# Two tiles instead of one fetched row by row by SyncE in every 24 groups of layer 1 (two-layer graph network, one core)

## The chip, the core and the metric

The kernel runs on one core of a Trainium2 chip. The metric is the device time of one execution in microseconds (us), the median of several runs. Five engines work side by side, each on its own list of instructions: TensorE (PE, with its weight loads PEld), VectorE (DVE), ScalarE (ACT), GpSimd (POOL) and SyncE (SP). They meet at semaphores. DMA transfers are issued by POOL and SP here and carried by 16 shared DMA engines.

## The reference

Two message passing layers over a graph of 6250 nodes with 128 features and 206250 edges, sorted by destination. Layer 0 is attention with 8 heads, layer 1 is attention by cosine. Cut to layer 1, which is the layer that changes:

```python
x = x + L0_gnn(edge_index, relu(layernorm(x)), Wq, Wk, Wv, gamma, beta, 8)
h = relu(layernorm(x))
norm  = ||h||                                   # per node
alpha = sum(h[row] * h[col]) / (norm[row] * norm[col]) * beta
alpha = exp(alpha - segment_max(alpha, row)[row])
alpha = alpha / segment_sum(alpha, row)[row]
x = x + segment_sum(alpha[:, None] * h[col], row)
```

For every edge the row `h[col]` has to be fetched from a table in memory by an index.

## The kernel before, in words

The sorted edges are cut into tiles of 128 edges, four tiles (GT = 4) to a group, 417 groups (GROUPS), 1668 tiles. Layer 0 (`layer0_edges`) and layer 1 (`layer1_edges`) both walk over the groups, one step for each group, and every engine walks by itself. In layer 1 the step of group i is:

- POOL (`gather_groups`, L918) fetches the 128 rows of each of its four tiles with one indirect DMA each into `h_rows` (the name `G` in the code), a ring of RING1 = 12 groups. It waits until ACT has copied the indices (`s_idx`) and until PE has used the group that lay in that place of the ring (`s_sum`).
- SP (`step`, L1462 to L1470) fetches at every fourth step the one-hot rows of four groups (`own`, L1467). Before it issues that DMA at step i it waits (L1466) until ACT has widened group i - 9 (`s_hotT`), which ACT does four steps ahead of its own step; so SP can be up to some 12 steps ahead of ACT, and no further. Then come the rows by hand (below), in the same step and on the same queue.
- ACT makes the logits from the cosines (L1507), copies the indices (L1483), scales the one-hot matrices (L1499) and widens `own` (L1494).
- PE multiplies: the queries (L1559), the transposed logits (L1568), the sums (L1578), the maxima (L1586).
- DVE makes the cosines (L1625), the running maxima (L1646, L1662), the differences, the one-hots (L1676) and adds the sums of group i - 9 (L1620).

One tile of every 24 groups (HAND1 = 24) is not gathered by POOL: tile 3 of the group with u = 23, u being the group's number modulo 24. Its 128 rows are fetched one at a time by SP (`hand_rows`, L1459: one DMA of 130 floats for each row) into the buffer `hand`, six rows (BYHAND1) in each of 22 steps, from the step with u = 10 to the step with u = 7 of the next 24. The numbers of the rows are loaded from `hand_ids` into registers, twelve at a time (L1455, 11 loads for a tile). Before the first of the 128 rows SP waits until ACT has emptied the buffer (`s_copied`). ACT copies `hand` into the ring (L1514) at its step u = 21, after waiting for all 128 rows, and DVE waits for that copy before the cosines of the group u = 23. Sixteen tiles (HANDS1 = 16) are fetched so. The first 24 groups have none, and the last tile is in group 407 (16 x 24 + 23).

The row numbers come from a small table in memory, `tile_names`, which SP writes at the start of layer 0 in four DMAs (L1021), before it loads the first rows of layer 0 (L1026). DVE's work in layer 0 starts once they have landed.

DVE, ACT, SP and POOL run their steps in loops whose bodies hold 24 groups in layer 1, PE's holds 12. The first 48 groups (24 or 12 on some engines) and the last are written out.

Of the kernel before, what the change touches and what calls it, by code (L numbers as in the profile page):

```python
# [15 lines left out]
P = 128  # L16
# [31 lines left out]
GT = 4  # L48
# [17 lines left out]
RING1 = 12  # L66
NEAR = 4
SLABS = -(-NT // P)
WHOLE = NT // P
# [6 lines left out]
FOUR = 4  # L76
QUADS = -(-GROUPS // FOUR)
HAND1 = 2 * RING1
HAND1_AT, BYHAND1 = 10, 6
BATCHES1 = -(-P // BYHAND1)  # L80
COPY1_AT = 21
HANDS1 = (GROUPS - HAND1) // HAND1
HAND_EVEN1 = sum(min(BYHAND1, P - BYHAND1 * b) for b in range(0, BATCHES1, 2))
PART = 7
# [4 lines left out]
TW = D + 2  # L89
# [4 lines left out]
i32 = mybir.dt.int32  # L94
# [757 lines left out]
def inside(g):  # L852

    return not isinstance(g, int) or 0 <= g < GROUPS
# [36 lines left out]

def by_hand(u, t, period):

    return period is not None and u == period - 1 and not (isinstance(t, int) and t == 0)


def gathers_of(t, u, ring, period):

    if period is None:
        return GT * (t + 1)  # L900
    each, now = GT * (period // ring), GT * (u // ring + 1)
    if u % ring < ring - 1 or isinstance(t, int) and t == 0:
        return each * t + now
    return (each - 1) * t + now + (u < period - 1)


def gather_groups(pool, ring, table, G, idx, s_idx, s_read, s_gat, s_go, period=None):
# [25 lines left out]
    nc.tensor.matmul(out, pick_row[:, g_u % FOUR, :], rows[:, h, :], start=True, stop=True).then_inc(s_spread, 1)  # L933


def hand_names(dram):

    per, step = P // GT, HAND1 * GT // (P // 4)
    rows = dram["names"].rearrange("k a c -> (k a) c")
    return rows[2 * step - 1:step * (HANDS1 + 1):step, :].rearrange("(o n) c -> o n c", o=1)  # L940


def layer0_edges(nc, mem, dram):

    with ExitStack() as ctx:
# [11 lines left out]
        G = sb("kv_rows", [P, RING0, GT, 2 * D])  # L957
# [4 lines left out]
        rows = sb("rows0", [FOUR, RING0 // FOUR, GE], bf16)  # L962
# [14 lines left out]
        s_ids = sem("s_ids0")  # L977
# [23 lines left out]
        s_sum = sem("s_sum0")  # L1001
# [4 lines left out]
        names = words.bitcast(i32)[:, 0:WHOLE, :]  # L1006
        loc_tiles = dram["loc_rows"].rearrange("g (j e) -> (g j) e", e=P)

        @block.sync
        def _(sp):  # L1010
            for n, (a, b) in enumerate(LOADS):
                sp.dma_start(words[:, a:min(b, WHOLE), :], words_in(dram, a, min(b, WHOLE))).then_inc(s_words[n], 16)
            sp.dma_start(words[0:REST, WHOLE, :], last_words(dram)).then_inc(s_words[n], 16)
            sp.wait_ge(s_bytile, 1)
            sp.dma_start(loc_tiles[0:whole * P, :].rearrange("(k t) e -> t k e", t=P), by_tile[:, 0:whole, :]).then_inc(s_stored, 16)
            sp.wait_ge(s_bytile, 2)
            sp.dma_start(loc_tiles[whole * P:NT, :], by_tile[0:rest, whole, :]).then_inc(s_stored, 16)
            sp.wait_ge(s_decoded, len(LOADS) + 1)
            for a in range(4):
                q = P // 4 * (a + 1) - 1  # L1020
                sp.dma_start(dram["names"][:, a, :].rearrange("(o k) c -> o k c", o=1), names[q:q + 1, :, :]).then_inc(s_ids, 16)  # L1021
            sp.wait_ge(s_ids, 16 * 4)
            sp.wait_ge(s_stored, 32)

            def load_rows(first, h, n):
                sp.dma_start(rows[0:n, h, :], dram["loc_rows"][ds(first, n), :]).then_inc(s_row[h], 16)  # L1026

            def step(i, u, t):
                last = isinstance(i, int) and i == GROUPS - 1
                if inside(i) and (u % FOUR == FOUR - 1 or last):  # L1030
                    q, h, n = RING0 // FOUR * t + u // FOUR, u // FOUR, u % FOUR + 1
                    sp.wait_ge(s_own, i + 1)
                    sp.sem_inc(s_go, 1)
                    sp.dma_start(own_quad(dram, q, n),
                                 own[:, FOUR * h:FOUR * h + n, :].rearrange("p g e -> p (g e)")).then_inc(s_kept[h], 16)
# [97 lines left out]
        def _(dve):  # L1133
# [3 lines left out]
            for n, (a, b) in enumerate(LOADS):  # L1137
                a, b = a * P, min(b * P, NT)
# [5 lines left out]
                                        ALU.add).then_inc(s_local, 1)  # L1144
            nc.vector.tensor_scalar(names, names, KEY, KEYS, ALU.logical_shift_right, ALU.bitwise_and).then_inc(s_decoded, 1)
            dve.wait_ge(s_part, 1)
            dve.wait_ge(s_ids, 16 * 4)

            block_4_back = BlockNumbers(nc, dve, blkid, RING0, IDS0, -4)

# [214 lines left out]
def layer1_edges(nc, mem, dram):  # L1365
# [3 lines left out]
    with ExitStack() as ctx:  # L1369
        def sb(name, shape, dt=f32):  # L1370
            return ctx.enter_context(nc.sbuf_tensor(name, shape, dt))

        def sem(name):
            return ctx.enter_context(nc.semaphore(name))
# [5 lines left out]
        PS = mem["psum"]  # L1380
        G = sb("h_rows", [P, RING1, GT, TW])
        own = sb("own1", [P, RING1, GE], u8)
        hand = sb("hand1", [P, TW])
        ids = sb("hand_ids1", [1, HANDS1 * P], i32)
        idx = sb("idx_ring1", [P, RING1, GT], i32)
        loc_b = sb("loc_b", [P, NT], bf16)
        iota_j = sb("iota_j", [P, P, GT], bf16)
# [24 lines left out]

        s_idx = sem("s_idx1")
        s_ids = sem("s_ids1")
        s_hand = [sem(f"s_hand1_{k}") for k in range(2)]
        s_copied = sem("s_copied1")
        s_gat = [sem(f"s_gat1_{k}") for k in range(RING1)]
        s_own = [sem(f"s_own_{k}") for k in range(RING1 // FOUR)]
# [24 lines left out]
        @block.sync  # L1443
        def _(sp):
            named = {}

            def hand_rows(u, t):
                n, b = (t, u - HAND1_AT) if u >= HAND1_AT else (t - 1, u + HAND1 - HAND1_AT)
                if b >= BATCHES1 or isinstance(n, int) and not 1 <= n <= HANDS1:
                    return  # L1450
                if b == 0:
                    need(sp, s_copied, n - 1)
                a = BYHAND1 * b
                if b % 2 == 0:
                    _, named[0] = nc.values_load_multi_w_load_instructions(  # L1455
                        ids[0:1, ds(P * n - P + a, min(2 * BYHAND1, P - a))], engines=[sp.engine], min_val=0,
                        max_val=NPAD - 1, skip_runtime_bounds_check_because="the numbers that the gathers use")
                for p in range(a, min(a + BYHAND1, P)):
                    sp.dma_start(hand[p:p + 1, :], dram["h1"][ds(named[0][p - a + BYHAND1 * (b % 2)], 1), :]  # L1459
                                 ).then_inc(s_hand[b % 2], 16)  # L1460

            def step(i, u, t):  # L1462
                if u % FOUR == 0 and inside(i):
                    n, k = min(FOUR, GROUPS - i) if isinstance(i, int) else FOUR, u % RING1
                    need(sp, s_hotT, i + n - RING1)
                    sp.sem_inc(s_go, 1)  # L1466
                    sp.dma_start(own[:, k:k + n, :].rearrange("p g e -> p (g e)"),  # L1467
                                 own_quad(dram, HAND1 // FOUR * t + u // FOUR, n)).then_inc(s_own[k // FOUR], 16)
                if inside(i):
                    hand_rows(u, t)  # L1470
            sp.dma_start(ids.rearrange("o (n c) -> o n c", c=P), hand_names(dram)).then_inc(s_ids, 16)
            sp.wait_ge(s_ids, 16)
            walk(sp, step, HAND1, first=0, drain=0, peel=2)

        @block.gpsimd
# [4 lines left out]
        def _(act):  # L1480
# [22 lines left out]
            def step(i, u, t):  # L1503
                if inside(i):
# [2 lines left out]
                    nc.scalar.activation(logit[:, u % RING1, :], cosb[:, u % SOON, :], ACT.Identity,  # L1507
                                         bias=cb[:, 1:2]).then_inc(s_logit, 1)
                    indices(i + RING1, u % RING1)
                if u == COPY1_AT and by_hand(HAND1 - 1, t, HAND1) and inside(i):  # L1510
                    act.wait_ge(s_hand[0], 16 * HAND_EVEN1 * t)
                    act.wait_ge(s_hand[1], 16 * (P - HAND_EVEN1) * t)
                    act.wait_ge(s_sum, HAND1 * t + HAND1 - RING1)
                    nc.scalar.copy(G[:, RING1 - 1, GT - 1, :], hand[:, :]).then_inc(s_copied, 1)  # L1514
                if inside(i - 7):
                    k = (u - 7) % SOON
                    act.wait_ge(s_below, i - 6)
# [74 lines left out]
        def _(dve):  # L1592
# [38 lines left out]
            def step(i, u, t):  # L1631
# [16 lines left out]
                if inside(i):  # L1648
                    dve.wait_ge(s_gat[u % RING1], 16 * gathers_of(t, u, RING1, HAND1))
                    if by_hand(u, t, HAND1):  # L1650
                        dve.wait_ge(s_copied, t)
                    dve.wait_ge(s_q, i + 1)
                    need(dve, s_logit, i + 1 - SOON)
                    need(dve, s_prod, i)
                    cosines(u, 0, GT // 2)
# [59 lines left out]
def program(nc, x, src, dst, wq, wk, wv, gamma, beta, cos_beta, out):  # L1715
# [2 lines left out]
        "offs": nc.dram_tensor("column_offsets", (2, NCHUNK, NBUK * STEP), bf16).ap(),  # L1718
        "loc_rows": nc.dram_tensor("loc_rows", (GROUPS, GE), bf16).ap(),
        "own": nc.dram_tensor("own_rows", (QUADS, P, FOUR * GE), u8).ap(),  # L1720
        "names": nc.dram_tensor("tile_names", (WHOLE, 4, P), i32).ap(),
# [48 lines left out]
```

## Time and profile before

| | |
|---|---|
| median of 3 runs | 4963.15 us (4962.42 to 4964.2) |
| the profiled execution | 4970.87 us |
| its span, first to last instruction | 4969.1 us |
| mean granted TensorE clock | 0.811 of full speed |
| layer 0's gathers | 592.1 to 2697.8 us |
| layer 1's gathers | from 2830.3 us, last one starts at 4905.0 us |
| busy in the span | PE 73%, PEld 60%, DVE 81%, ACT 47%, POOL 71% |

An engine's busy time leaves out its register, branch, semaphore and DMA-issuing instructions; the whole of SP is of that kind, so it has no busy share, and its load has to be read from the times between its DMAs. A figure such as "L1459 ... x2048" in a row counts instructions of one line of the kernel. "Idle before" names what an engine's next instruction came after.

### The profile page before, as it was taken

How to read it: one execution, taken by the hardware profiler on the slowest of the kernel's cores; microseconds unless marked ns; L12 is line 12 of the kernel's file. 1: busy time of each engine (PE TensorE's matmuls, PEld its weight loads, DVE VectorE, ACT ScalarE, POOL GpSimd, SP SyncE). 2: the span in 40 equal slices, each digit the busy share in tenths (PEclk: the TensorE clock that was granted, in tenths of full speed). 3: DMA queues.
4: the chain of work that ended last, by engine and by line, in shares of the span. 5: the costliest groups of instructions: out<-in, count | busy, mean ns of one | idle time of the engine just before them, and what ended most of it. 6: DMA issues, size and time to landing. Idle time of an engine off the chain costs nothing. (4 is left out here: it accounts for less than half of the span.)

```text
span 4969.1 us, 105610 instructions
## 1 busy us (share of the span) xinstructions
PE 3613.5 (73%) x21325; PEld 2995.8 (60%) x21326; DVE 4026.9 (81%) x12159; ACT 2349.1 (47%) x8244; POOL 3505.2 (71%) x3613
## 2 busy tenths in 40 slices
PE   5777577877777777777775177777778777777776
PEld 1444455655555655555664077777777777667775
DVE  7999688888888888888888677777777777777776
ACT  3999511111111111111111676776766777777774
POOL 1667677777777777777775177777777777777773
PEclk7999687677777777777776588998988999999887
DMA  1000134334333333333332222222222222222222
GB/s 50 21 29 28 43 114 119 117 116 117 117 117 119 117 117 117 117 117 119 117 117 86 46 69 68 68 68 68 69 67 68 68 69 68 67 68 70 68 68 54
DMA packets 206558, 412.52 MB, mean 83 GB/s; under 512 B 66973, under 2 KB 97984, under 8 KB 206206
## 3 DMA queue, kind: packets, MB, share of 16 engines
q0 software_dynamic: 136384, 329.69, 24.5%
q1 hardware_dynamic: 67986, 75.70, 4.8%
q10 hardware_dynamic: 1836, 4.03, 0.3%
q14 instruction: 326, 2.67, 0.2%
q8 instruction: 26, 0.43, 0.0%
HBM read 363.48 MB, written 42.44 MB: 82 GB/s over the span
## 5 line engine op out<-in xcount | busy, mean ns | idle before, releaser
L918 POOL DMA_INDIRECT h_rows<-h_table,idx_ring x1652 | 1572.1, 952 | 635.2 <-issue 487.8
L918 POOL DMA_INDIRECT kv_rows<-kv_table,idx_ring x1668 | 1598.5, 958 | 513.8 <-issue 506.3
L1127 PE MATMUL psum<-vx,hot 128*128 128x136 f32 x3336 | 820.9, 387 | 413.3 <-DVE acc L1158 400.2
L1127 PEld LDWEIGHTS psum<-vx,hot 128*128 128x128 f32 x3336 | 628.7, 260 | 584.2 <-DVE acc L1158 555.7
L1080 ACT ACTIVATE vx<-clip 128x32 f32<-128x32 f32 x417 | 95.8, 230 | 1741.5 <-DVE clip L1200 1741.5
L1620 DVE SCALAR_TENSOR_TENSOR h_sb<-h_sb,corr,psum 128x129 f32 x1668 | 582.3, 349 | 391.0 <-PE psum L1578 145.6
L1116 PE MATMUL psum<-q_sb,hotT 128*128 x3336 | 679.7, 367 | 75.6 <-DVE prod L1173 65.3
L1116 PEld LDWEIGHTS psum<-q_sb,hotT 128*128 128x128 f32 x3336 | 578.1, 261 | 210.8 <-issue 210.8
L1568 PE MATMUL psum<-ident,hotl 128*128 128x128 f32 x1668 | 303.4, 311 | 493.4 <-DVE highs L1646 490.6
L1158 DVE TENSOR_TENSOR acc<-acc,psum 128x136 f32 x1668 | 488.6, 293 | 156.5 <-issue 32.2
L1625 DVE SCALAR_TENSOR_TENSOR prod<-psum,h_rows 128x128 f32<-128x128 f32 x1668 | 511.1, 344 | 118.7 <-DMA h_rows<-h_table,idx_ring 112.9
L1499 ACT ACTIVATE hotl<-hot,logit 128x128 f32<-128x128 bf16 x1668 | 538.8, 394 | 0.0
L1568 PEld LDWEIGHTS psum<-ident,hotl 128*128 128x128 f32 x1668 | 199.2, 155 | 561.9 <-issue 423.7
L1499 ACT ACTIVATE hotw<-hot,wgt 128x128 f32<-128x128 bf16 x1668 | 536.5, 393 | 0.2
L1578 PE MATMUL psum<-h_rows,hotw 128*128 128x129 f32 x3336 | 521.2, 307 | 3.6 <-DVE h_sb L1620 3.1
L1559 PE MATMUL psum<-q_sb,acc 128*128 x3336 | 509.6, 299 | 17.6 <-DVEq L1608 5.7
L1578 PEld LDWEIGHTS psum<-h_rows,hotw 128*128 128x128 f32 x3336 | 485.1, 223 | 5.3 <-issue 3.7
L1586 PEld LDWEIGHTS psum<-tops,acc 128*128 128x128 f32 x3336 | 455.2, 211 | 0.0
L1559 PEld LDWEIGHTS psum<-q_sb,acc 128*128 128x128 f32 x3336 | 437.0, 204 | 26.3 <-issue 22.6
L1586 PE MATMUL psum<-tops,acc 128*128 128x1 f32 x3336 | 437.8, 252 | 0.0
L1507 ACT ACTIVATE logit<-cosb,cb_sb 128x4 f32<-128x4 f32 x417 | 124.1, 298 | 619.4 <-DVE prod L1625 613.4
L616 ACT ACTIVATE ends<-is_place,pk_now 128x96 f32<-128x96 bf16 x972 | 368.0, 463 | 57.6 <-DVE is_place L802 57.0
(224 smaller groups left out, 5441.7 us busy)
## 6 DMA issues: line engine op xcount, KB each, us to landing
hand<-h_table SPq DMA_DIRECT2D x2048, 0.5 KB
kv_rows<-kv_table,idx_ring POOLq DMA_INDIRECT x1668, 2.9
own_rows<-own SPq DMA_DIRECT2D x104, 256.0 KB, 2.6
own<-own_rows SPq DMA_DIRECT2D x104, 256.0 KB
h_rows<-h_table,idx_ring POOLq DMA_INDIRECT x1652
kv_table<-kv SPq DMA_DIRECT2D x21, 256.0 KB, 2.2
out<-q_sb SPq DMA_DIRECT2D x2, 1536.0 KB
h_sb<-h_now SPq DMA_DIRECT2D x21, 128.0 KB, 2.0
```

Source lines behind the costliest of these rows:

```text
L616: last = nc.scalar.activation(to_place[:, k, c, :], is_place[:, k, :, c], ACT.Copy, scale=pk_now[:, r, BATCH * b + c:BATCH * b + c + 1])
L918: pool.indirect_dma_start(out=G[:, k, j, :], out_offset=None, in_=table, in_offset=bass.IndirectOffsetOnAxis(ap=idx[:, k, j:j + 1], axis=0 ...
L1116: last = nc.tensor.matmul(Q_ps[k][:, j * P:(j + 1) * P], hotT[:, k, j * P:(j + 1) * P], q_sb[:, ds(blks[j], 1), :].rearrange("p o f -> p ( ...
L1127: last = nc.tensor.matmul(S_ps[j // HALF][:, j % HALF, :], hot[:, k, j * P:(j + 1) * P], vx[:, k, j, :], start=True, stop=True)
L1158: nc.vector.tensor_tensor(sums, sums, S_ps[h // HALF][:, h % HALF, :], ALU.add).then_inc(s_acc, 1)
L1499: last = nc.scalar.activation(out[:, j * P:(j + 1) * P], hot[:, u, :, j], ACT.Copy, scale=scale[:, j:j + 1])
L1559: last = nc.tensor.matmul(Q_ps[k][:, j * P:(j + 1) * P], hotT[:, (u + 1) % RING1, j * P:(j + 1) * P], q_sb[:, ds(blks[j], 1), :].rearrange ...
L1568: last = nc.tensor.transpose(L_ps[u % 2][:, j * P:(j + 1) * P], hotl[:, (u - 2) % TRIO, j * P:(j + 1) * P], ident[:, :])
L1578: last = nc.tensor.matmul(S_ps[j // HALF][:, j % HALF, :], hotw[:, (u - 8) % TRIO, j * P:(j + 1) * P], G[:, (u - 8) % RING1, j, 0:AW1], st ...
L1586: last = nc.tensor.matmul(E_ps[:, j:j + 1], hotT[:, n, j * P:(j + 1) * P], tops[:, n, j, 1:2], start=True, stop=True)
L1620: nc.vector.scalar_tensor_tensor(sums, sums, corr[:, (u - 9) % RING1, h:h + 1], S_ps[h // HALF][:, h % HALF, :], ALU.mult, ALU.add).then_i ...
L1625: last = nc.vector.scalar_tensor_tensor(prod[:, j * P:(j + 1) * P], Q_ps[u % 2][:, j * P:(j + 1) * P], G[:, u % RING1, j, D + 1:TW], G[:, ...
```

## The change

Two tiles of every 24 groups are fetched by SP, tile 3 of the group u = 11 and tile 3 of the group u = 23, each into a buffer of its own (`hand[:, half, :]`). The first (half 0) is fetched from the step u = 22 of the 24 before to the step u = 19, and ACT copies it at its step u = 9. The second (half 1) is fetched as before and copied at u = 21. So in 20 of 24 steps SP issues six rows for each half, twelve in all, and in 4 (u = 8, 9, 20, 21) six. POOL gathers 1636 tiles in place of 1652. `tile_names` has eight rows to a block in place of four, written by eight DMAs in place of four, and layer 1 starts with two loads of row numbers in place of one, both waited for.

```diff
-HAND1_AT, BYHAND1 = 10, 6
+HAND1_AT, BYHAND1 = (-2, 10), 6
-COPY1_AT = 21
+COPY1_AT = (9, 21)
+NAMED = 8
...
 def by_hand(u, t, period):
-    return period is not None and u == period - 1 and not (isinstance(t, int) and t == 0)
+    return period is not None and u % (period // 2) == period // 2 - 1 and not (isinstance(t, int) and t == 0)
...
-    return (each - 1) * t + now + (u < period - 1)
+    return (each - 2) * t + now + (u < period - 1)
...
-            for a in range(4):
-                q = P // 4 * (a + 1) - 1
+            for a in range(NAMED):
+                q = P // NAMED * (a + 1) - 1
                 sp.dma_start(dram["names"][:, a, :].rearrange("(o k) c -> o k c", o=1), names[q:q + 1, :, :]).then_inc(s_ids, 16)
...
-            def hand_rows(u, t):
-                n, b = (t, u - HAND1_AT) if u >= HAND1_AT else (t - 1, u + HAND1 - HAND1_AT)
+            def hand_rows(u, t, half):
+                if u >= HAND1_AT[half] % HAND1:
+                    n, b = t + 1 - half, u - HAND1_AT[half] % HAND1
+                else:
+                    n, b = t - half, u + HAND1 - HAND1_AT[half] % HAND1
                 if b >= BATCHES1 or isinstance(n, int) and not 1 <= n <= HANDS1:
                     return
                 if b == 0:
-                    need(sp, s_copied, n - 1)
+                    need(sp, s_copied, 2 * n - 3 + half)
...
                 for p in range(a, min(a + BYHAND1, P)):
-                    sp.dma_start(hand[p:p + 1, :], dram["h1"][ds(named[0][p - a + BYHAND1 * (b % 2)], 1), :]
-                                 ).then_inc(s_hand[b % 2], 16)
+                    sp.dma_start(hand[p:p + 1, half, :], dram["h1"][ds(named[half][p - a + BYHAND1 * (b % 2)], 1), :]
+                                 ).then_inc(s_hand[half][b % 2], 16)
...
                 if inside(i):
-                    hand_rows(u, t)
-            sp.dma_start(ids.rearrange("o (n c) -> o n c", c=P), hand_names(dram)).then_inc(s_ids, 16)
-            sp.wait_ge(s_ids, 16)
+                    for half in range(2):
+                        hand_rows(u, t, half)
+            for half in range(2):
+                sp.dma_start(ids[32 * half:32 * half + 1, :].rearrange("o (n c) -> o n c", c=P), hand_names(dram, half)).then_inc(s_ids, 16)
+            sp.wait_ge(s_ids, 32)
...
-                if u == COPY1_AT and by_hand(HAND1 - 1, t, HAND1) and inside(i):
-                    act.wait_ge(s_hand[0], 16 * HAND_EVEN1 * t)
-                    act.wait_ge(s_hand[1], 16 * (P - HAND_EVEN1) * t)
-                    act.wait_ge(s_sum, HAND1 * t + HAND1 - RING1)
-                    nc.scalar.copy(G[:, RING1 - 1, GT - 1, :], hand[:, :]).then_inc(s_copied, 1)
+                if u in COPY1_AT and by_hand(HAND1 - 1, t, HAND1) and inside(i):
+                    half = COPY1_AT.index(u)
+                    act.wait_ge(s_hand[half][0], 16 * HAND_EVEN1 * t)
+                    act.wait_ge(s_hand[half][1], 16 * (P - HAND_EVEN1) * t)
+                    act.wait_ge(s_sum, HAND1 * t + RING1 * half)
+                    nc.scalar.copy(G[:, RING1 - 1, GT - 1, :], hand[:, half, :]).then_inc(s_copied, 1)
...
                     if by_hand(u, t, HAND1):
-                        dve.wait_ge(s_copied, t)
+                        dve.wait_ge(s_copied, 2 * t - (u < RING1))
```

## Rows read from the trace of the kernel before

**Rows 1.** Groups by line, 2750 to 4950 us (layer 1)

```profile
line engine op names shapes xcount | busy us, mean ns | idle before us <-releasers
L918 POOL DMA_INDIRECT h_rows<-h_table,idx_ring x1652 | 1572.1, 952 | 635.2 <-issue 487.8 <-ACT idx_ring L1483 133.1 <-PE psum L1578 14.3
...
L1514 ACT COPY h_rows<-hand 128x130 f32<-128x130 f32 x16 | 4.8, 300 | 0.0
```

**Rows 2.** Waits by engine, 2900 to 4800 us: total, times, longest

```profile
POOL h_rows L918 <- issue: 446.0, 1462, 0.3
POOL h_rows L918 <- PE psum L1578: 14.3, 47, 0.3
...
DVE prod L1625 <- DMA h_rows<-h_table,idx_ring: 100.4, 142, 1.6
DVE h_sb L1620 <- issue: 87.8, 72, 4.1
```

**Rows 3.** Timeline of POOL at the end of layer 1

```profile
4901.24 0.95 POOL L918 DMA_INDIRECT h_rows<-h_table,idx_ring  x1 [0.30 <-issue]
4902.49 0.94 POOL L918 DMA_INDIRECT h_rows<-h_table,idx_ring  x1 [0.30 <-issue]
...
4905.00 0.95 POOL L918 DMA_INDIRECT h_rows<-h_table,idx_ring  x1 [0.30 <-issue]
```

**Rows 4.** Instructions that touch the tile `hand`: count, ns min/median/max, first and last start

```profile
L1459 SPq DMA_DIRECT2D hand<-h_table x2048: 224/228/299, 2939.6 to 4839.1; - x187
L1514 ACT COPY h_rows<-hand x16: 283/301/302, 3064.9 to 4855.3; 128x130 f32<-128x130 f32 x16
```

**Rows 5.** Timeline of SP over one loop body (24 groups); only DMAs are shown

```profile
3595.47 0.36 SPq L1467 DMA_DIRECT2D own<-own_rows  x1
3597.06 11.18 SPq L1459 DMA_DIRECT2D hand<-h_table  x24
3615.59 0.36 SPq L1467 DMA_DIRECT2D own<-own_rows  x1
3617.23 11.17 SPq L1459 DMA_DIRECT2D hand<-h_table  x24
...
3664.26 4.76 SPq L1459 DMA_DIRECT2D hand<-h_table  x12
3675.91 0.36 SPq L1467 DMA_DIRECT2D own<-own_rows  x1
3677.50 10.82 SPq L1459 DMA_DIRECT2D hand<-h_table  x24
```

**Rows 6.** Instructions of L1455, L1459 and the loop's L845 on SP, 3608.4 to 3730.2 us

```profile
L1455 SPq TENSOR_LOAD <-hand_ids x11: 684/913/929, 3616.1 to 3723.8; - x11
...
L1459 SPq FUSED_REGOPS  x128: 37/37/37, 3617.1 to 3729.6; - x128
L1459 SPq MOVE hand<-h_table x128: 29/29/37, 3617.2 to 3729.7; - x128
L1459 SPq DMA_DIRECT2D hand<-h_table x128: 224/228/282, 3617.2 to 3729.8; - x128
...
L845 SPq COMPARE_BRANCH  x2: 53/53/53, 3608.4 to 3730.1; - x2
L845 SPq FUSED_REGOPS  x2: 50/50/50, 3611.2 to 3732.6; - x2
```

**Rows 7.** Waits of SP's own queue, 3608.4 to 3730.2 us

```profile
SPq L1466 <- ACT acc L1494: 42.1, 6, 11.1
SPq L1455 <- ACT h_rows L1514: 7.4, 1, 7.4
```

**Rows 8.** Timeline of SP where layer 1 starts

```profile
2829.24 0.58 SPq L1471 DMA_DIRECT2D hand_ids<-tile_names  x1
2831.38 106.95 SPq L1467 DMA_DIRECT2D own<-own_rows  x9
2939.57 5.25 SPq L1459 DMA_DIRECT2D hand<-h_table  x12
```

**Rows 9.** Timeline of DVE around the end of its loop body

```profile
3431.98 0.34 DVE L1625 SCALAR_TENSOR_TENSOR prod<-psum,h_rows 128x128 f32<-128x128 f32 x1
...
3436.44 0.84 DVE L1620 SCALAR_TENSOR_TENSOR h_sb<-h_sb,corr,psum 128x129 f32 x2 [3.70 <-issue]
```

**Rows 10.** Timeline of DVE: the first cosine of steps that follow one another

```profile
3426.79 0.34 DVE L1625 SCALAR_TENSOR_TENSOR prod<-psum,h_rows 128x128 f32<-128x128 f32 x1
...
3431.03 0.34 DVE L1625 SCALAR_TENSOR_TENSOR prod<-psum,h_rows 128x128 f32<-128x128 f32 x1
...
3448.72 0.34 DVE L1625 SCALAR_TENSOR_TENSOR prod<-psum,h_rows 128x128 f32<-128x128 f32 x1
...
3454.77 0.34 DVE L1625 SCALAR_TENSOR_TENSOR prod<-psum,h_rows 128x128 f32<-128x128 f32 x1
...
3460.90 0.34 DVE L1625 SCALAR_TENSOR_TENSOR prod<-psum,h_rows 128x128 f32<-128x128 f32 x1
```

**Rows 11.** Busy time in stretches: PE, PEld, DVE, ACT, POOL, granted clock, DMA share, GB/s

```profile
3426.80:3431.00 4.20, 3.31 (x28) 3.15 (x28) 3.65 (x18) 3.69 (x15) 3.01 (x4) 1.00 0.21 49
3449.30:3461.30 12.00, 12.00 (x57) 11.64 (x56) 7.41 (x35) 6.99 (x27) 8.95 (x11) 0.50 0.24 59
3486.60:3544.60 58.00, 42.77 (x359) 40.38 (x358) 46.23 (x211) 43.74 (x165) 43.97 (x47) 1.00 0.27 68
```

**Rows 12.** Timeline of DVE: the first cosines of the last group

```profile
4908.60 0.34 DVE L1625 SCALAR_TENSOR_TENSOR prod<-psum,h_rows 128x128 f32<-128x128 f32 x1
```

**Rows 13.** Timeline where layer 0 starts, and its first 32 gathers (592 to 634 us)

```profile
601.84 3.29 SPq L1021 DMA_DIRECT2D tile_names<-hot  x4
...
606.96 0.68 SPq L1026 DMA_DIRECT2D rows<-loc_rows  x2
...
623.50 0.68 DVE L1186 TENSOR_TENSOR vx<-kv_rows,vx 128x512 f32<-128x512 f32 x1
...
L918 POOL DMA_INDIRECT kv_rows<-kv_table,idx_ring x32: 945/949/1461, 592.1 to 632.3; - x32
```

**Rows 14.** Timeline where layer 1 starts: ACT's first widening of `own`

```profile
2848.76 2.18 ACT L1494 CAST acc<-own 128x512 f32<-128x512 uint8 x4 [18.09 <-PE psum L1547]
```

**Rows 15.** Page, part 6: DMAs of SP whose landing is seen (us in the last column)

```profile
kv_table<-kv SPq DMA_DIRECT2D x21, 256.0 KB, 2.2
...
h_sb<-h_now SPq DMA_DIRECT2D x21, 128.0 KB, 2.0
```

More of the change, by code:

```diff
@@ L933, in spread_row, with hand_names @@
     nc.tensor.matmul(out, pick_row[:, g_u % FOUR, :], rows[:, h, :], start=True, stop=True).then_inc(s_spread, 1)
-def hand_names(dram):
-    per, step = P // GT, HAND1 * GT // (P // 4)
+def hand_names(dram, half):
+    step = HAND1 * GT // (P // NAMED)
     rows = dram["names"].rearrange("k a c -> (k a) c")
-    return rows[2 * step - 1:step * (HANDS1 + 1):step, :].rearrange("(o n) c -> o n c", o=1)
+    first = step + step // 2 * (half + 1) - 1
+    return rows[first:first + step * (HANDS1 - 1) + 1:step, :].rearrange("(o n) c -> o n c", o=1)
 def layer0_edges(nc, mem, dram):
@@ L1018, in _ @@
             sp.wait_ge(s_decoded, len(LOADS) + 1)
-            for a in range(4):
-                q = P // 4 * (a + 1) - 1
+            for a in range(NAMED):
+                q = P // NAMED * (a + 1) - 1
                 sp.dma_start(dram["names"][:, a, :].rearrange("(o k) c -> o k c", o=1), names[q:q + 1, :, :]).then_inc(s_ids, 16)
-            sp.wait_ge(s_ids, 16 * 4)
+            sp.wait_ge(s_ids, 16 * NAMED)
             sp.wait_ge(s_stored, 32)
@@ L1146, in _ @@
             dve.wait_ge(s_part, 1)
-            dve.wait_ge(s_ids, 16 * 4)
+            dve.wait_ge(s_ids, 16 * NAMED)
             block_4_back = BlockNumbers(nc, dve, blkid, RING0, IDS0, -4)
@@ L1382, in layer1_edges @@
         own = sb("own1", [P, RING1, GE], u8)
-        hand = sb("hand1", [P, TW])
-        ids = sb("hand_ids1", [1, HANDS1 * P], i32)
+        hand = sb("hand1", [P, 2, TW])
+        ids = sb("hand_ids1", [33, HANDS1 * P], i32)
         idx = sb("idx_ring1", [P, RING1, GT], i32)
@@ L1414, in layer1_edges @@
         s_ids = sem("s_ids1")
-        s_hand = [sem(f"s_hand1_{k}") for k in range(2)]
+        s_hand = [[sem(f"s_hand1_{h}_{k}") for k in range(2)] for h in range(2)]
         s_copied = sem("s_copied1")
@@ L1451, in hand_rows @@
                 if b == 0:
-                    need(sp, s_copied, n - 1)
+                    need(sp, s_copied, 2 * n - 3 + half)
                 a = BYHAND1 * b
                 if b % 2 == 0:
-                    _, named[0] = nc.values_load_multi_w_load_instructions(
-                        ids[0:1, ds(P * n - P + a, min(2 * BYHAND1, P - a))], engines=[sp.engine], min_val=0,
+                    _, named[half] = nc.values_load_multi_w_load_instructions(
+                        ids[32 * half:32 * half + 1, ds(P * n - P + a, min(2 * BYHAND1, P - a))], engines=[sp.engine], min_val=0,
                         max_val=NPAD - 1, skip_runtime_bounds_check_because="the numbers that the gathers use")
                 for p in range(a, min(a + BYHAND1, P)):
-                    sp.dma_start(hand[p:p + 1, :], dram["h1"][ds(named[0][p - a + BYHAND1 * (b % 2)], 1), :]
-                                 ).then_inc(s_hand[b % 2], 16)
+                    sp.dma_start(hand[p:p + 1, half, :], dram["h1"][ds(named[half][p - a + BYHAND1 * (b % 2)], 1), :]
+                                 ).then_inc(s_hand[half][b % 2], 16)
             def step(i, u, t):
@@ L1720, in program @@
         "own": nc.dram_tensor("own_rows", (QUADS, P, FOUR * GE), u8).ap(),
-        "names": nc.dram_tensor("tile_names", (WHOLE, 4, P), i32).ap(),
+        "names": nc.dram_tensor("tile_names", (WHOLE, NAMED, P), i32).ap(),
         "kv": nc.dram_tensor("kv_table", (NPAD, 2 * D), f32).ap(),
```

## The prediction

> **What bounds the kernel now.** The change lives in layer 1, so the page's averages over the whole span (DVE 81%, POOL 71%) say little; I read the views of layer 1 alone, in this order. First the groups by line [rows 1]: POOL's gathers are the costliest group, 1652 of 952 ns. Then the waits [rows 2]: POOL's idle time is 1462 pieces that end in "issue" and are at most 0.3 us long, and the pieces put down to PE are also 0.3 us, the same as the bare step from one gather to the next. So POOL never really waits. The end of its timeline shows the beat: a gather every 1.253 us, (4905.00 - 4901.24) / 3, up to the last one [rows 3]. A group costs POOL 4 x 1.253 = 5.01 us. The others can go faster: with data at hand DVE's steps follow each other in 4.24 us (3426.79 to 3431.03), and its waits in the middle of a step are 100 us on the gathers [rows 2, 10]. The copies of `hand` confirm the beat: 16 of them from 3064.9 to 4855.3, so 119.4 us for 24 groups, against 95 x 1.253 = 119.0 us for POOL's gathers [rows 4]. Before the change POOL sets the pace, and each gather that it does not make is worth 1.25 us as long as nothing else becomes slower than it.
>
> **The second list to read is SP's, which no busy share shows.** One row by hand is a DMA instruction of 228 ns [rows 4], but it has company. Twelve rows without a load of numbers in between take from 3664.26 for 4.76 us to the end of the last, so (4.76 - 0.23) / 11 = 0.412 us a row [rows 5]. Twenty-four rows with one load in between take 10.82 us, so the load costs 10.82 - 0.23 - 23 x 0.412 = 1.1 us, 0.91 of it the load itself [rows 5, 6]. Some such stretches take 11.18 us; about 0.36 us is now and then lost between two rows. A tile is then 128 x 0.412 + 11 x 1.1 = 64.8 us. The same comes out from the whole loop body: from branch to branch 3730.1 - 3608.4 = 121.7 us, of which SP waited 42.1 + 7.4 = 49.5 [rows 6, 7]; it worked for 72.2 us. Six `own` DMAs at about 0.63 us with their registers and semaphore (0.36 is the DMA [rows 5]; an estimate) are 3.8, the branch is 2.8 (3608.4 to 3611.2 [rows 6]), which leaves 65.6 for the 128 rows. I take 65.6, with 64.8 and 66.5 as its bounds. SP is busy for 60% of the body.
>
> **The change part by part.**
>
> *POOL gathers sixteen tiles fewer.* 16 x 1.253 = 20.0 us off POOL's list. A body of 24 groups is then 94 x 1.253 = 117.8 us for POOL.
>
> *SP fetches a second tile in every body.* It adds 65.6 us to 72.2: 137.8 us of SP's own work in 24 groups, against 117.8 of POOL. There is nothing to hide this behind: SP's queue is one list, and the 256 row DMAs, the 22 loads of numbers, the `own` DMAs and the branch all stand in it one behind the other. SP falls behind by 20 us in every body unless everything else slows to it.
>
> *Where the lateness goes.* ACT's copy at u = 9 needs the rows that SP issues up to its step u = 19, the copy at u = 21 those up to its step u = 31: SP has to be ten steps ahead. The wait on `s_hotT` allows about twelve. So it has a margin of two steps, some 10 us, and then ACT waits at each copy. Behind the waiting copy on ACT are the scaled one-hots of this step and all later ones, so PE and DVE stop, then POOL when its ring is full. The price of SP's list is paid in full by all.
>
> *The sum.* SP issues its ninth `own` DMA (step 32) at 2938.3 [rows 8], still held back by ACT; the six rows of each of the steps 22 to 31, about 3 us, fit between. Its steps 32 to 43 hold 128 rows and two further `own` DMAs, 65.6 + 1.3 us, so the last row of the first tile is issued at 3005.2 and lands some 2 us later, by the nearest DMAs of SP whose landing is seen, 2.0 to 2.2 us [rows 15]: 3007.3. ACT undelayed would be at that copy (its step 33) 12 steps before the first copy of before, 3064.9 - 59.7 = 3005.2 [rows 4]. So the wait begins with the very first copy. From here each copy follows SP. The first and the 31st copy lie 15 bodies apart: 15 x 137.8 = 2067, so the 31st (step 393) is at 5074. SP has then only 68 rows left (37 us), and the 32nd copy is not late. From the 31st copy to the cosines of the last group are 23 steps at DVE's free pace, 23 x 4.24 = 97.5, with one stall at the end of the loop body of 3.7 [rows 9], and some three steps at the lower clock after the wait, 1.9 us more each, 5.6 (4.24 us a step at 2.4 GHz, granted clock 1.00; 6.1 us at 1.2 GHz, clock 0.50 [rows 10, 11]): 106.8. POOL, which ran four groups ahead during the wait, has 20 groups left, 100 us, and isn't the limit. Then the tail as before, 4969.1 - 4908.6 = 60.5 us [rows 12]. The span ends at 5074 + 107 + 60.5 = 5241.5, so 272.4 us later than 4969.1. The profiled execution took 4970.87 us, 1.8 over its span and 7.7 over the median of the runs, 4963.15; the difference is added to the median: 5235.5. I add 3 us for the steps at which SP, on coming from a wait of ACT, finds the widening of `own` not yet done (below), and say 5239.
>
> *What is free.* The four further stores of `tile_names` are 4 x 0.8 = 3.3 us by those of before, on SP ahead of layer 0's first rows [rows 13]. DVE's first `vx` would come 3.3 us later than 624.2; POOL needs it for its 33rd gather, after 632.3 + 1.25 = 633.6, 9.4 us later. So they cost 0, and 3.3 us without that cover. The second load of `hand_ids` (0.58 us [rows 8]) lies ahead of the first `own`, which ACT widens only at 2848.8, 17 us after its issue [rows 14]: 0. Sixteen more copies on ACT, 0.3 us each, 4.8 in all [rows 1], fall into its idle time: 0. The copy waits for the sums of the group that had the place before, at the same distance as before: 0.
>
> *A rule beside the rows.* What SP adds is issue time alone: 256 x 0.412 = 105 us of a body without any load [rows 5]. The Trainium skill, page "DMA: Bandwidth & Descriptors", section "Issuing engines are not separate DMA queues", calls the time that a sequencer takes to initiate a DMA usually small relative to the DMA itself. By that rule the second tile would be free and only POOL's saving would remain (the third rival below gives its time). With rows of 520 bytes the trace does not bear it out, and I go by the rows.
>
> **The rivals.**
>
> 1. *SP sets the pace* as summed: 5239.
>
> 2. *The wait costs the clock too.* At each copy PE stands idle for some 5 to 15 us. In the trace of before the granted clock is at 0.50 in stretches between the quick ones, also while PE is 12.00 of 12.00 us busy, and a step then takes 6.1 us [rows 10, 11]. If it stayed there all the time, 12 steps would be 73 us and 24 with the stall 150, more than SP's 137.8: 15 x 12 = 180 us more, some 5420. For it speaks that the low clock occurs in this layer although its work never stops for long [rows 9, 11]; against it that after two or three slow steps the clock is at 1.00 for 58 us of steady work [rows 11], and only 20% of the time is waiting here. A milder form is likelier: three or four slow steps after each copy make ACT late for SP's wait on `s_hotT`. SP reaches the `own` DMA of step u = 24 after 19 us (12 rows in two light steps, 24 in two heavy ones), ACT has to finish step u = 11 by then, 2 + 3 + 2 x 6.1 = 17 us. Two more slow microseconds would be paid 30 times, 60 us: 5300.
>
> 3. *SP keeps up* (the other side). If a row cost SP only its three instructions of 228, 37 and 29 ns, 0.29 us [rows 6], a body would be 256 x 0.29 + 22 x 0.91 + 6.6 = 101 us, below POOL's 117.8, and the time would be 4963.15 - 20.0 = 4943. It decides below (117.8 - 6.6 - 22 x 1.1) / 256 = 0.34 us a row. The rows show 0.412 back to back, with nothing to wait for in between [rows 5], in 128 of 128 rows of a body. Only if the gaps came from something that twelve rows in a row would not meet could it be so.
>
> 4. *SP is the limit but dearer*: registers that hold 24 numbers in place of 12 need a further instruction, or row DMAs queue up behind each other. 0.03 us a row is 4096 x 0.03 = 123 us; I see no row that calls for it.
>
> **How the numbers follow.** SP's pace as summed, in its own range of 5205 to 5275 (0.9 us a tile either way is 15 x 2 x 0.9 = 27 us, and 5 us for start and end): 0.72. The same with late `own` or slow clock in part, up to 5310: 0.12. Full low clock or dearer rows, 5310 to 5450: 0.08. Rows somewhat cheaper than the sum, 5000 to 5205: 0.04. SP keeps up: 0.04, of which 0.03 below the bound. The prediction is 5239, the range 5205 to 5310. A change of 0.2% (10 us) is about what a measurement of this kernel can tell from none. Faster 0.03, same 0.01, slower 0.96.
>
> **What would show it.** In the changed kernel the waits of SP's queue vanish between the first copy and the last, and the body lasts about 137.8 us; the copies of `hand` are 32, from 3007 to some 5127, and ACT's idle time before L1514, 0.0 now, is some 10 us a copy on the average, some 300 in all. POOL gets real waits, over 0.3 us, put down to PE's sums. SP's rows still follow each other in 0.41 us. POOL's busy time falls by 16 gathers. Layer 0 keeps its times. Wrong would be: rows at under 0.34 us; or an ACT that does not stand at L1514, which would mean that a part of the rows isn't needed where I think; or steps of 6.1 us throughout, the second rival.

## The result, and the profile after

The changed kernel takes 5228.37 us (median of five runs, 5223.69 to 5228.95), the kernel before 4964.2 us beside it: ratio 1.053, interval 1.0519 to 1.0541. It is slower by 264 us; 5239 was predicted, in 5205 to 5310. The profiled execution has a span of 5227.1 us.

The page of the changed kernel, part 1 (busy time, share of the span, instructions). By this view every engine has less to do than before in proportion; nothing in it is a bound.

```profile
span 5227.1 us, 112148 instructions
PE 3683.8 (70%) x21325; PEld 3064.7 (59%) x21326; DVE 4022.9 (77%) x12159; ACT 2351.2 (45%) x8260; POOL 3493.4 (67%) x3597
```

The timeline of SP over one loop body (only DMAs are shown) answers [rows 5]:

```profile
3575.07 0.36 SPq L1472 DMA_DIRECT2D own<-own_rows  x1
3576.68 23.26 SPq L1464 DMA_DIRECT2D hand<-h_table  x48
3600.28 0.36 SPq L1472 DMA_DIRECT2D own<-own_rows  x1
3601.86 21.44 SPq L1464 DMA_DIRECT2D hand<-h_table  x44
3623.55 0.37 SPq L1472 DMA_DIRECT2D own<-own_rows  x1
3625.14 17.34 SPq L1464 DMA_DIRECT2D hand<-h_table  x36
3642.81 0.36 SPq L1472 DMA_DIRECT2D own<-own_rows  x1
3644.39 23.12 SPq L1464 DMA_DIRECT2D hand<-h_table  x48
```

In [rows 5] there were holes of several microseconds between the end of a stretch of rows and the next `own`; here the next `own` is issued 0.25 to 0.34 us after the last row. SP's queue is full. Its instructions in the same body (count, ns min/median/max, first and last start) answer [rows 6]:

```profile
L1464 SPq DMA_DIRECT2D hand<-h_table x256: 224/228/277, 3576.7 to 3709.7; - x128
L1460 SPq TENSOR_LOAD <-hand_ids x22: 687/912/1093, 3575.6 to 3701.6; - x22
L846 SPq COMPARE_BRANCH  x2: 53/53/53, 3572.1 to 3710.0; - x2
```

The body lasts 3710.0 - 3572.1 = 137.9 us, with the same 228 ns for a row DMA. The waits of SP's queue from 2900 to 5200 us are now 18.3 us in all, 4 times, three before the first copy of `hand` and one behind the 31st; there is none from 3000 to 4900 us, where [rows 7] had 49.5 us in one body:

```profile
SPq L1471 <- ACT acc L1501: 18.3, 4, 7.2
```

Who waits instead stands in the waits of the engines, 2900 to 5050 us (total, times, longest), against [rows 2]:

```profile
DVE h_sb L1628 <- PE psum L1586: 486.1, 300, 20.5
PEld psum L1576 <- ACT hotl L1506: 296.3, 28, 19.6
POOL h_rows L919 <- PE psum L1586: 266.1, 92, 14.8
ACT h_rows L1522 <- issue: 248.0, 15, 19.6
ACT h_rows L1522 <- DMA hand<-h_table: 53.1, 13, 6.3
```

The last two rows are ACT at its copies, 301 us. "Issue" in the first of them is ACT idle with no releaser that the view can name; at 13 further copies the view names the rows of `hand`. The rows above them are the same wait handed on: PE has no scaled one-hots, DVE no sums, POOL no free place in its ring. That can be followed at one copy, on POOL, ACT and DVE:

```profile
3615.29 0.95 POOL L919 DMA_INDIRECT h_rows<-h_table,idx_ring  x1 [0.31 <-issue]
3630.13 0.95 POOL L919 DMA_INDIRECT h_rows<-h_table,idx_ring  x1 [13.89 <-PE psum L1586]
...
3624.32 0.30 ACT L1522 COPY h_rows<-hand 128x130 f32<-128x130 f32 x1 [18.91 <-issue]
3689.34 0.30 ACT L1522 COPY h_rows<-hand 128x130 f32<-128x130 f32 x1 [1.87 <-DMA hand<-h_table]
...
3629.46 0.84 DVE L1628 SCALAR_TENSOR_TENSOR h_sb<-h_sb,corr,psum 128x129 f32 x2 [19.82 <-PE psum L1586]
```

The rows that the first of these copies needs end with the stretch of 44 rows above, at 3601.86 + 21.44 = 3623.30, and the copy is at 3624.32, 1.0 us later. POOL, which never stands for more than 0.3 us in [rows 3], stands for 13.9 us here. All copies in the view of the tile `hand`, against [rows 4]:

```profile
L1464 SPq DMA_DIRECT2D hand<-h_table x4096: 224/228/300, 2877.6 to 5104.6; - x196
L1522 ACT COPY h_rows<-hand x32: 284/299/301, 3003.1 to 5117.3; 128x130 f32<-128x130 f32 x32
```

### The profile page after: what moved, and what is told of

It reads as the page before. It is cut to its first block and busy times, and to the rows that moved or that the text cites. A ratio compares the mean times of both kernels' runs of the same rounds, so it can differ in the third digit from the quotient of the medians.

```text
span 5227.1 us, 112148 instructions
## 1 busy us (share of the span) xinstructions
PE 3683.8 (70%) x21325; PEld 3064.7 (59%) x21326; DVE 4022.9 (77%) x12159; ACT 2351.2 (45%) x8260; POOL 3493.4 (67%) x3597
## 5 line engine op out<-in xcount | busy, mean ns | idle before, releaser
L1576 PE MATMUL psum<-ident,hotl 128*128 128x128 f32 x1668 | 318.7, 323 | 673.3 <-DVE highs L1654 374.3
L1586 PE MATMUL psum<-h_rows,hotw 128*128 128x129 f32 x3336 | 549.8, 318 | 9.3 <-ACT hotw L1506 6.2
L1567 PE MATMUL psum<-q_sb,acc 128*128 x3336 | 538.8, 311 | 10.6 <-DVEq L1616 5.7
L1586 PEld LDWEIGHTS psum<-h_rows,hotw 128*128 128x128 f32 x3336 | 509.8, 233 | 21.6 <-issue 20.0
L1594 PEld LDWEIGHTS psum<-tops,acc 128*128 128x128 f32 x3336 | 475.3, 219 | 0.0
L1567 PEld LDWEIGHTS psum<-q_sb,acc 128*128 128x128 f32 x3336 | 466.1, 216 | 13.6 <-issue 13.1
L1594 PE MATMUL psum<-tops,acc 128*128 128x1 f32 x3336 | 456.3, 258 | 0.0
```

What stands on the lines that cost most here:

```text
L1567: last = nc.tensor.matmul(Q_ps[k][:, j * P:(j + 1) * P], hotT[:, (u + 1) % RING1, j * P:(j + 1) * P], q_sb[:, ds(blks[j], 1), :].rearrange ...
L1576: last = nc.tensor.transpose(L_ps[u % 2][:, j * P:(j + 1) * P], hotl[:, (u - 2) % TRIO, j * P:(j + 1) * P], ident[:, :])
L1586: last = nc.tensor.matmul(S_ps[j // HALF][:, j % HALF, :], hotw[:, (u - 8) % TRIO, j * P:(j + 1) * P], G[:, (u - 8) % RING1, j, 0:AW1], st ...
L1594: last = nc.tensor.matmul(E_ps[:, j:j + 1], hotT[:, n, j * P:(j + 1) * P], tops[:, n, j, 1:2], start=True, stop=True)
```

## The experiments

Ten kernels were run; each ratio is to the kernel before, run beside it on the same chip (4960.5 us for the first four, 4961.3 for the next four, 4968.7 for the last two).

**E1, POOL gathers everything.** The change's SP part alone.

```diff
-    return (each - 2) * t + now + (u < period - 1)
+    return (each - 1) * t + now + (u < period - 1)
...
-        hand = by_hand(u, t, period)
+        hand = by_hand(u, t, period) and u == period - 1
...
+        spare = sb("spare1", [P, TW])
...
-                    nc.scalar.copy(G[:, RING1 - 1, GT - 1, :], hand[:, half, :]).then_inc(s_copied, 1)
+                    nc.scalar.copy(G[:, RING1 - 1, GT - 1, :] if half else spare[:, :], hand[:, half, :]).then_inc(s_copied, 1)
```

> SP fetches both tiles as in the change, but POOL gathers the u = 11 tile too (1652 gathers) and ACT copies the first half's buffer into a spare tile, so only POOL's saving of 16 x 1.253 = 20.0 us is undone. Theory (SP's own list of 138.0 us in 24 groups sets the pace): no change against the changed kernel, 5228 us, body still 138.0 us, since POOL has 119 us of work in it. Rival (the loss comes from POOL or from its waits on the ring): 20 us more, 5248 us, or another pace.

Measured: 5227.53 us, ratio 1.0539 (1.0523 to 1.0555), the same as the change. The body of SP is 3706.3 - 3568.3 = 138.0 us. POOL's 16 gathers more cost nothing, so in the changed kernel POOL's saving of 20 us brings nothing. The whole loss comes with SP's second tile.

**E2, half of the rows.** SP fetches 65 rows of the first half's tile. The other 63 keep a constant, and ACT waits for the 65; that tile's right values are left out.

```diff
-                for p in range(a, min(a + BYHAND1, P)):
+                for p in range(a, min(a + (BYHAND1 if half else 3), P)):
...
```

> Of the first half's tile SP fetches three rows in each of 22 steps instead of six (65 rows of 128; the others keep a constant, so the work of 63 rows is left out); loads of numbers, copies and waits stay. Theory: SP's body is 138.0 - 63 x 0.412 = 112.0 us, below POOL's 94 x 1.253 = 117.8, so POOL sets the pace again and its saving shows: 4964 - 20 = 4944 us, no idle time of ACT before L1522 to speak of. Rival (the copy at u = 9, its waits or the two buffers cost the time, not the number of rows): stays near 5228 us. Rival (a fixed part of the lateness is left): between, 5000 to 5100.

Measured: 4943.49 us, ratio 0.9966 (0.9953 to 0.9979), against 4944 expected (4940.5, if the 20 us are taken off the kernel before beside it). In the waits from 2900 to 4800 us POOL is back at its own step of 0.3 us and no wait at the copy is among the groups:

```profile
POOL h_rows L919 <- issue: 444.1, 1457, 0.3
POOL h_rows L919 <- PE psum L1588: 17.1, 56, 0.3
```

Both buffers, both copies and all 22 loads are still there. The copies of `hand` lie 117.9 us apart for 24 steps (3003.6 to 4831.6 us for 15.5 times as many), against 137.9 in the changed kernel. So none of these costs the time; 63 rows in each body do.

**E3, short rows.** The same number of DMAs, 8 bytes each; the rest of the buffer keeps a constant, so the right values of these tiles are left out.

```diff
-                    sp.dma_start(hand[p:p + 1, half, :], dram["h1"][ds(named[half][p - a + BYHAND1 * (b % 2)], 1), :]
+                    sp.dma_start(hand[p:p + 1, half, 0:2], dram["h1"][ds(named[half][p - a + BYHAND1 * (b % 2)], 1), 0:2]
...
```

> Every row by hand moves 8 bytes instead of 520 (two floats; the rest of the buffer keeps a constant, so the values of these tiles are left out); the number of DMAs, loads and waits is that of the change. Theory (issue on SP's sequencer counts): as the change, 5228 us within 5, rows still 0.412 us apart, body 138 us. Rival (the transfers themselves or their landing are the limit): clearly faster, down to 4944.

Measured: 5230.72 us, ratio 1.0544 (1.0528 to 1.056). SP's timeline is that of the changed kernel to a few hundredths of a microsecond:

```profile
3572.19 0.36 SPq L1473 DMA_DIRECT2D own<-own_rows  x1
3573.81 23.25 SPq L1465 DMA_DIRECT2D hand<-h_table  x48
3597.40 0.36 SPq L1473 DMA_DIRECT2D own<-own_rows  x1
3598.99 21.41 SPq L1465 DMA_DIRECT2D hand<-h_table  x44
```

So the bytes are not what fills SP's list. E3 keeps the number of DMAs, and by itself it can't tell SP's instructions from a limit on that number; E7 below can, since there all 256 rows of a body are still fetched.

**E4, the names alone.** The kernel before with eight stores of names.

```diff
-            for a in range(4):
-                q = P // 4 * (a + 1) - 1
+            for a in range(NAMED):
+                q = P // NAMED * (a + 1) - 1
...
```

> The kernel before with eight stores of the tile names instead of four and nothing else of the change. Theory: 0 us, hidden behind POOL's first 32 gathers, 9 us of slack. Rival: 3.3 us more, 4967.

Measured: 4961.26 us, ratio 1.0003 (0.9994 to 1.0012). The stores do take 3 us more on SP (6.32 us for eight in its timeline, 3.29 for four in [rows 13]), and nobody waits for them.

```profile
599.90 6.32 SPq L1022 DMA_DIRECT2D tile_names<-hot  x8
607.78 0.63 SPq L1027 DMA_DIRECT2D rows<-loc_rows  x2
```

**E5, four rows of six.** As E2 with a 4 in the place of the 3 (86 rows).

> As the run with three rows in a step, but four rows of the first half in each step (86 of 128 rows; 42 are left out). Theory: SP's body is 138.0 - 42 x 0.412 = 120.7 us, just over POOL's 117.8 and over the 119.4 of the kernel before, so SP still sets the pace by a little: by 15 bodies of 17.3 us less than the changed kernel, 5228 - 260 = 4968 us, the break-even with the kernel before (4961) a little below four rows. Rival (a threshold at which the whole loss comes at once): 5228. Rival (the queue can run ahead between the copies, so four are free): 4944.

Measured: 4980.42 us, ratio 1.0037 (1.0023 to 1.0051), 12 us over the expectation. There is no threshold at which the whole loss comes at once, and the queue does not hide four rows either. The pace is the expected one: from the first copy to the 31st, 15 bodies apart, it is 1804.2 us, so 120.3 a body, against 120.7 expected and 137.4 in the changed kernel.

```profile
3000.33 0.30 ACT L1524 COPY h_rows<-hand 128x130 f32<-128x130 f32 x1
...
4804.50 0.30 ACT L1524 COPY h_rows<-hand 128x130 f32<-128x130 f32 x1 [0.77 <-issue]
```

Most of the 12 us lie behind the 31st copy. The expectation took only the bodies off and kept the changed kernel's end, in which DVE runs ahead at its free pace: there 102.2 us pass from the 31st copy to the cosines of the last group, here 113.0 (4804.5 to 4917.5), with POOL at 5.0 us a group to the end. Both lists wait a little for each other on the way (SP's waits from 2900 to 4900 us, ACT's to 4800):

```profile
SPq L1472 <- ACT acc L1503: 45.9, 19, 11.0
...
ACT h_rows L1524 <- DMA hand<-h_table: 67.3, 14, 6.4
```

Of SP's 45.9 us only 17.3 lie behind 3000 us, about 1 us in a body, and the pace shows no loss by them.

**E6, longer loads.** Up to 24 numbers in a load.

```diff
-            named = {}
+            named, start = {}, {}
...
-                if b % 2 == 0:
+                if b == 0 or u % 4 == 0:
+                    start[half], m = a, min(BYHAND1 * (4 - u % 4), P - a)
                     _, named[half] = nc.values_load_multi_w_load_instructions(
-                        ids[32 * half:32 * half + 1, ds(P * n - P + a, min(2 * BYHAND1, P - a))], engines=[sp.engine], min_val=0,
+                        ids[32 * half:32 * half + 1, ds(P * n - P + a, m)], engines=[sp.engine], min_val=0,
...
```

> The whole change, but SP loads its row numbers up to 24 at a time instead of 12: 6 loads for a tile instead of 11. A load of 12 takes 0.91 us and one of 8 0.68, so 0.057 a number and 0.23 and some gaps fixed. Theory: five fixed parts of about 0.43 us less for each tile, 4.3 us a body, 133.7 us, times 15: 65 us less, 5163 us. Rival (only the row DMAs count, or loads overlap them): 5228.

Measured: 5160.5 us, ratio 1.04 (1.0384 to 1.0415), against 5163 expected. The body is 3685.3 - 3551.4 = 133.9 us. The load's price was right:

```profile
L1461 SPq TENSOR_LOAD <-hand_ids x192: 911/1585/1680, 2874.7 to 5027.1; - x192
```

A load of 24 takes 1585 ns, one of 12 took 912. The loads are a part of SP's list like the rows, and 4 us less in a body are some 65 us less in the kernel (1.053 less 1.040 of 4964 us).

**E7 and E8, ACT issues a part.** All rows are fetched. ACT issues the first 44 (E7) or 66 (E8) rows of the first half's tile, two or three in each of 22 steps, the numbers loaded every four steps; SP keeps 84 or 62. E7 in short (ACT_ROWS = 2, SP_ROWS = 4):

```diff
+                by = BYHAND1 if half else SP_ROWS
+                lo = 0 if half else ACT_ROWS * BATCHES1
+                a = lo + by * b
...
+            def assist(u, t):
+                n, b = (t + 1, u - COPY1_AT[0] - 1) if u > COPY1_AT[0] else (t, u + HAND1 - COPY1_AT[0] - 1)
...
+                for k in range(ACT_ROWS):
+                    p = ACT_ROWS * b + k
+                    act.dma_start(hand[p:p + 1, 0, :], dram["h1"][ds(held["rows"][p - ACT_ROWS * held["first"]], 1), :]
+                                  ).then_inc(s_assist, 16)
...
```

> The whole change, with all rows fetched, but 44 of the 128 rows of the first half are issued by ACT, two in each of 22 of its steps, with a load of up to eight numbers every four steps; SP keeps 84 of that tile. Theory: SP's body is 65.6 + 84 x 0.412 + 11 x 0.87 + 6.6 = 116.4 us, under POOL's 117.8; ACT gets 44 x 0.41 + 6 x 0.9 = 23 us more in a body in which its free time was some 30. If that fits: POOL's saving shows, 4942 us. Rival (ACT stands in the chain of every step, and 0.8 us more in it makes the steps longer than POOL's 4.9 us): 4970 to 5100.

> As the run before with three rows in each of 22 of ACT's steps (66 rows; SP keeps 62). Theory: SP's body 65.6 + 62 x 0.412 + 11 x 0.8 + 6.6 = 106.5 us, well under POOL; ACT gets 33 us more, all of its free time, and becomes the slowest: its step is 3.7 + 1.2 + 0.2 = 5.1 us in 22 of 24, so 4950 to 5020 us. Rival (ACT hides it): 4942.

Measured: E7 4949.76 us, ratio 0.9974 (0.9963 to 0.9985); E8 4948.97 us, ratio 0.9973 (0.9963 to 0.9983). Both are faster than the kernel before, by 0.3%, and a little above the 4942 of a pace that is POOL's alone. All 256 rows of a body are fetched again, and the loss is gone: what was full was SP's list. E7's profiled execution took 4963.8 us, the longest of its seven (the median is 4949.8), so its waits show more than the median has. In it a rest of the old wait is left, SP in turn waits 43 us for ACT's widening (3000 to 4800 us), and 24 steps take 119.2 us from copy to copy (3004.4 to 4733.0 us for 14.5 times as many) against POOL's 117.8. The waits of E7, 2900 to 4800 us:

```profile
ACT h_rows L1552 <- DMA hand<-h_table: 60.1, 13, 5.7
```

In E8 no copy waits. ACT has 165 us of idle time in front of its widening, which stands right behind the row DMAs in its list; the view names no releaser, so that this is the time of its own DMA instructions and loads is a reading. Against the expectation, ACT did not become the slowest: 24 steps take 118.1 us (3002.3 to 4833.0 us for 15.5 times as many), POOL's pace within 0.3 us, and the time is 1 us below the expected range. In the same stretch:

```profile
ACT acc L1528 <- issue: 165.3, 94, 2.4
```

And E8's instructions that touch `hand`:

```profile
L1515 ACTq DMA_DIRECT2D hand<-h_table x1056: 220/221/552, 2889.2 to 4765.6; - x176
```

**E9 and E10, ACT's part and the longer loads together.** The edits of E6 and E7, of E6 and E8.

> All rows fetched; ACT issues 44 rows of the first half and SP loads its numbers up to 24 (16 for the first half) at a time. Theory: SP's body 116.4 us less 2.2 for the second half's loads and about 2 for the first's, 112 us, 6 us under POOL's 117.8, so the copies wait hardly any more (60 us in the run with ACT's help alone) and POOL sets the pace: 4942 us. Rival (what is left over 4942 there comes from ACT's own longer steps): as there, 4949.

> As the run before with 66 rows issued by ACT. Theory: SP has still more room that nobody needs, 103 us; ACT waits for no row already in the run with three rows alone, so no change against it, 4948 us, 5 us above POOL's pace from ACT's work. Rival (SP's room still counts): 4942.

Measured: E9 4952.37 us beside 4968.7 of before, ratio 0.9969 (0.9957 to 0.9981); E10 4958.14 us, ratio 0.9977 (0.9968 to 0.9986). On this chip the kernel before is 7 us longer, so the ratios are to be read. POOL's pace alone would be 4968.7 - 20.0 = 4948.7 here; E9 is 3.7 us above it. The expectation for E9 (0.9960) and its rival (as E7, 0.9974) both lie in its interval, so E9 does not decide between them. E10 is as E8 (0.9973), as was expected, and not at POOL's pace. In E9's profile the wait at the copy is gone and POOL is back at 0.3 us:

```profile
POOL h_rows L921 <- issue: 440.1, 1442, 0.3
POOL h_rows L921 <- PE psum L1619: 20.7, 68, 0.3
```

The four ratios of E7 to E10 lie in each other's intervals: which of them is best was not settled. That of E2, 0.9966, lies in those of E7, E8 and E9, and 0.0002 below that of E10. POOL's saving of 20 us is a ratio of 0.9960 and lies in the interval of E9 and E2, outside that of E7, E8 and E10 by 0.0003 to 0.0008.

## Why the prediction was right

**POOL's pace and its saving** (1.253 us a gather, 20.0 us). E2 shows it: with SP out of the way 24 steps take 117.9 us (117.8 predicted), and the time is 4943.5 us, 17 us under the kernel before beside it, interval 10 to 23. In the change itself it is worth nothing, as E1 shows.

**The price of SP's list.** 137.8 us for a body was the term that carries the forecast; 137.9 to 138.0 was measured. It held because it was taken from the whole body of before, SP's time less its waits [rows 6, 7], and not from the 228 ns of the DMA alone. Rival 3, the sum of the three instructions of a row, would have given 101 us; the gaps between them are part of the price. The trace had shown them, and nothing in E3 or the change made them smaller.

**The way of the wait.** Nothing absorbs it, but it begins one copy later than was predicted. The first copy was expected to wait, at 3007.3 us. It stands at 3003.1 with no idle time before it; the last of its rows ends at 3001.5, and in E2, where SP has room, the same copy is at 3003.6. The wait begins with the second copy and is found at 29 of the 32. The 31st stands at 5064.7 (5074), the 32nd, which does not wait, at 5117.3.

```profile
3003.09 0.30 ACT L1522 COPY h_rows<-hand 128x130 f32<-128x130 f32 x1
3072.66 0.30 ACT L1522 COPY h_rows<-hand 128x130 f32<-128x130 f32 x1 [9.12 <-issue]
...
5064.74 0.30 ACT L1522 COPY h_rows<-hand 128x130 f32<-128x130 f32 x1 [8.53 <-issue]
```

ACT's wait at the copies is 310 us in all, 300 predicted. From the 31st copy to the cosines of the last group, 5166.9, it took 102 us (107 predicted), and from there to the end 60.2 (60.5).

**Where 11 us went.** The span is 5227.1 us, where 5241.5 was summed. The first copy came 4 us earlier, at ACT's own pace, so the 2 us that the sum gave a row to land played no part there; at the later copies a row is used 1.0 us after the end of its DMA instruction. The 15 bodies took 5064.7 - 3003.1 = 2061.6 us, not 2067: the thirteen in the middle took 137.9 us each, but the first and the last 134.8 and 133.8, since no jump back of SP's loop falls into them, which the sum had charged. The last stretch was 4.6 us shorter: the three slow steps that the sum had put behind the copy did not come (the granted clock is 0.91 up to 5095 us and 1.00 from there to 5138). POOL, which "isn't the limit" there by the prediction, was nearly that: its last gather starts at 5163.7 us and the cosines of the last group 3.3 us later, 3.6 in the kernel before [rows 3, 12]. The 3 us added for SP's own waits weren't needed either, since SP had none between 3000 and 4900 us. The other way went the step from span to median, for which 6 us were taken off as in the kernel before; here the median lies 1.3 us above the span. So some luck is in the total: the chain was summed 17 us too long, and the step to the median took 7 of them back.

**The second rival was nearer than the total tells.** The waits at the two copies of a body were taken as alike, some 10 us. In the body shown they are 18.9 and 1.9 us, and 17.5 and 4.1 on the average of the thirteen bodies in the middle. Most of this difference is not the clock's. By the times of the copies, SP itself needs 72.9 us from the last row for the copy at u = 9 to that for the copy at u = 21, with 134 rows and the end of its loop in between, and 65.0 us for the other half of the body, with 122 rows. ACT's and DVE's loops end in the half that follows the long wait, and there DVE stands for 3.7 us, as in [rows 9]. Of the difference between the waits, 17.0 us in the body shown and 13.4 on the average, these two leave 5.4 and under 2 us. In the body shown the rest goes with the clock: in the half behind the long wait four of DVE's steps take 5.0 to 6.1 us in place of 4.24, and the granted clock is lower than in the other half (columns: PE, PEld, DVE, ACT, POOL, clock, DMA share, GB/s):

```profile
3624.30:3687.50 63.20, 50.29 (x316) 47.93 (x316) 41.22 (x187) 41.96 (x157) 40.01 (x42) 0.77 0.23 58
3689.30:3743.90 54.60, 42.27 (x330) 40.01 (x328) 43.89 (x202) 41.99 (x157) 41.02 (x44) 0.94 0.29 69
```

It is not so in every body: in the next three the two halves have 0.83 and 0.88, 0.84 and 0.80, 0.77 and 0.80. The slow steps do not follow the copy at once. The stretch from 3629 to 3642 us has 0.89, that from 3642 to 3660 has 0.69 with PE busy for 16.2 of 18 us, where steps at the higher of the two levels, 2.4 GHz, and at 1.2 GHz are mixed:

```profile
3605.00:3629.00 24.00, 5.12 (x33) 4.53 (x32) 4.10 (x19) 5.06 (x21) 8.50 (x9) 0.58 0.16 40
3629.00:3642.00 13.00, 7.91 (x56) 7.48 (x56) 7.49 (x34) 6.47 (x25) 7.57 (x8) 0.89 0.19 45
3642.00:3660.00 18.00, 16.22 (x96) 15.69 (x95) 12.09 (x53) 12.54 (x48) 11.87 (x13) 0.69 0.23 61
```

The 12 steps from one copy to the wait before the next took 3689.34 - 1.87 - 3624.32 = 63.2 us, and SP needed 65.0. One more slow step (1.9 us) would have used this margin up, and any further one would have been paid. The mean granted clock from 3000 to 5000 us is 0.82, from 3000 to 4800 us in the kernel before 0.90; it cost nothing only because SP was slower still.

**Free as said:** the names (E4), the second load of `hand_ids`, the 16 copies of ACT. What was mis-sized in the experiments is E5, by 12 us: its body was right, but the end of layer 1 is 11 us longer where the kernel comes to it at POOL's pace than where it comes to it held up by SP.

The rule of the Trainium skill, page "DMA: Bandwidth & Descriptors", section "Issuing engines are not separate DMA queues", that the time to initiate a DMA is usually small relative to the DMA, gives no price for a list of such rows. A row takes 0.41 us of SP's list and is used 1.0 us after the end of its instruction; but SP issues the next row without waiting for it, so here the issue times add up and set the pace, and by E3 the size of the transfer does not matter. The same section says that issuing from several engines saves the sequencer's time alone, and with this the runs agree: that is what E7 and E8 gain.

## What to carry to other kernels

An engine that only issues has no busy share, so before work is moved to it, take one loop body of its queue, subtract its waits, and compare the rest with the pace of the kernel; here 72 of 119 us looked like room and a second tile of 65.6 us did not fit. Price a moved instruction by the distance from one to the next in a stretch without waits, its register work and the loads of its numbers included, not by its own duration. When the slower list is only a little over the pace, split it: a third of the second tile on another issuing queue turned 5% slower into 0.3% faster.

## What the runs showed of the hardware

A row DMA of 8 bytes costs SP as much as one of 520 bytes: 228 ns for the instruction and the same 48 rows in 23.25 and 23.26 us. ACT issues the same row in 221 to 224 ns. A load of numbers into SP's registers took 0.69 us for 8, 0.91 for 12 and 1.59 for 24, so it grows by 0.056 to 0.057 us a number over some 0.23 us. SP's loop took 2.7 us from the branch at its end to the next instruction (3572.1 to 3574.8 us), and DVE stood for 3.7 us at the end of its own. The mean granted clock of layer 1 was 0.90 before and 0.82 in the changed kernel, where ACT waits for 310 us; how much of this the waits cause, no run here shows.
